# A rebuilt middle stage in a fused adaptive-layernorm block with two attentions: quotients token by token, centring on ScalarE

## What is computed

```python
phiQ, phiK = favor(Q), favor(K)                 # [B, H, T, 64]
KV, Ksum = einsum('bhtm,bhtd->bhmd', phiK, V), phiK.sum(axis=2)
out_heads = einsum('bhtm,bhmd->bhtd', phiQ, KV) / (einsum('bhtm,bhm->bht', phiQ, Ksum)[..., None] + EPS)
x = x + ga * (merge(out_heads) @ Wo.T + bo)
h = layernorm(x) * (1 + cb) + sb                # second norm, scale and shift
xn = layernorm(h) * norm_w + norm_b             # third norm, per expert
q, k, v = (xn[..., :m] @ w[:, :m].T + b for w, b in ((q_w, q_b), (k_w, k_b), (v_w, v_b)))
x = x + gb * (h + softmax(q @ k.T / 16) @ v @ o_w.T + o_b)
```

## Time and profile before

| | |
|---|---|
| median of 3 runs | 2007.24 us (2006.68 to 2007.88) |
| the profiled execution's own time | 2007.16 us |
| its span, and mean granted TensorE clock | 2005.4 us, 0.93 of 2.4 GHz |
| busy share: TensorE, VectorE, GpSimd, ScalarE | 87%, 72%, 59%, 54% |
| batch 1's middle stage, from the first L1188 to the last L911's end | 683.14 to 778.75 us: 95.6 us |
| batch 1's first score of the softmax attention | 794.51 us |

### The profile page before, as it was taken

One profiled execution on the slowest core, in us unless ns is written; L12 is line 12 of the kernel. 1 busy time (PEld: TensorE's weight loads), 2 busy tenths in 40 slices (PEclk: granted clock), 3 DMA queues, 4 the chain that ended last, 5 costly groups with the idle time before them and its releaser, 6 DMA issues.

```text
span 2005.4 us, 31471 instructions
## 1 busy us (share of the span) xinstructions
PE 1750.5 (87%) x11520; PEld 997.9 (50%) x11520; DVE 1450.5 (72%) x2617; ACT 1083.1 (54%) x1998; POOL 1179.5 (59%) x974
## 2 busy tenths in 40 slices
PE   5698869999899886999979977799997988599997
PEld 3576434444377543444447744344435764344443
DVE  4686777777478577777648857777766876787774
ACT  0586333656578432566648823266665863336564
POOL 0685354666768346566768723666676853546666
PEclk8898978999999897999989989899998989889999
DMA  4000043001110025101020003500111000430011
GB/s 126 1 2 1 18 158 85 17 11 39 53 33 2 1 72 167 30 9 48 1 85 2 2 1 117 140 12 17 41 34 52 2 2 0 171 89 16 12 37 43
DMA packets 55714, 87.56 MB, mean 44 GB/s; under 512 B 13188, under 2 KB 32004, under 8 KB 52868
## 3 DMA queue, kind: packets, MB, share of 16 engines
q1 hardware_dynamic: 55560, 85.54, 14.5%
HBM read 49.68 MB, written 35.70 MB: 43 GB/s over the span
## 4 chain that ended last, share of the span: by engine, by line
PE 65%; DVE 14%; ACT 10%; issue 4%; POOL 3%; DMA 2%; SPq 2%; POOLq 0%; ACTq 0%; DVEq 0%
PE PS L1175 12%; PE PS L1300 11%; PE PS L1288 9%; PE PS L1313 5%; PE PS L1069 5%; DVE MXP L861 4%; PE PS L1096 3%; PE PS L1077 3%; PE PS L1218 3%; PE PS L1106 3%; ACT HT L525 2%; ACT HTR L528 2%; PE PS L1245 2%; DVE QKS L911 2%; ACT PHIQ L563 2%
## 5 line engine op out<-in xcount | busy, mean ns | idle before, releaser
L498 POOL TENSOR_TENSOR TS<-PR 128x1024 f32<-128x1024 f32 (+1 forms) x256 | 573.1, 2239 | 336.7 <-ACT PR L664 336.7
L861 DVE TENSOR_REDUCE MXP<-PS 128x1 f32<-128x512 f32 x960 | 598.0, 680 | 202.7 <-PE PS L1175 199.3
L664 ACT ACTIVATE PR<-PS 128x512 f32<-128x512 f32 x960 | 504.8, 602 | 425.9 <-PE PS L1288 422.4
L1175 PE MATMUL PS<-KOP,QOP 96*128 96x512 f32 x960 | 422.8, 460 | 45.1 <-DMA KOP<-k_scr 34.2
L1288 PE MATMUL PS<-QOP,KOP 97*128 97x512 f32 x960 | 379.4, 409 | 18.1 <-ACT PR L664 12.7
L1175 PEld LDWEIGHTS PS<-KOP,QOP 96*128 96x128 f32 x960 | 190.7, 200 | 300.3 <-DVE MXP L861 174.7
L1300 PE MATMUL PS<-PR,V 128*32 128x512 f32 x1920 | 273.1, 606 | 0.0
L1288 PEld LDWEIGHTS PS<-QOP,KOP 97*128 97x128 f32 x960 | 181.3, 192 | 85.6 <-ACT PR L664 50.2
L445 POOL TENSOR_TENSOR RSTD<-VE,minus_half 128x4 f32<-128x4 f32 x32 | 33.9, 1060 | 237.6 <-DVE VE L758 237.6
L1313 PE MATMUL PS<-TS,ones 128*32 128x512 f32 x960 | 133.2, 593 | 5.4 <-POOL TS L498 5.4
L1069 PE MATMUL PS<-W1T,HTR 128*128 128x512 f32 x384 | 115.1, 438 | 21.2 <-POOL HTR L402 21.0
(11 more groups left out here) (144 smaller groups left out, 2691.0 us busy)
## 6 DMA issues: line engine op xcount, KB each, us to landing
KOP<-k_scr SPq DMA_DIRECT2D x84, 256.0 KB, 6.0
k_scr<-QKS SPq DMA_DIRECT2D x64, 256.0 KB, 2.8
QOP<-q_scr SPq DMA_DIRECT2D x180, 64.0 KB, 2.0
q_scr<-QKS SPq DMA_DIRECT2D x40, 256.0 KB, 2.8
X<-in_L_attn_x_dram SPq DMA_DIRECT2D x16, 512.0 KB, 4.8
out_dram<-X SPq DMA_DIRECT2D x16, 512.0 KB, 3.1
QOP<-MXT SPq DMA_DIRECT2D x240, 0.5 KB
KOP<-k_scr SPq DMA_DIRECT2D x48, 64.0 KB, 2.0
```

Of the source, the lines that this page charges most:

```text
L498: g.tensor_tensor(sums(k)[:, 0:len(stage)], pair[:, :, 0], pair[:, :, 1], ALU.add).then_inc(S["psum_t"], 1)
L664: a.activation(PR[:, k % 2, w, q], bank(score_bank(p, n, w, q)), ACT.Exp).then_inc(S["ex"], 1)
L861: v.tensor_reduce(MXP[:, u % 2, i, kc:kc + 1], bank(max_bank(p)), AX.X, ALU.max).then_inc(S["am_rd"], 1)
L1175: mm(bank(max_bank(p)), QOP[0:96, u % QS6, i * P:(i + 1) * P], KOP[0:96, h % KS6, kc * CH:(kc + 1) * CH], start=True, stop=True).then_inc( ...
```

## The change

Only the middle stage, its edges and a small part of the setup are changed.

- Quotients: the features become the stationary operand. For each tile of 128 tokens, eight matmuls (one for each pair of heads) with 34 moving columns (`KVW`: 32 for the numerators, 2 for the denominators) give numerators and denominators with the tokens on the partitions. VectorE takes reciprocals straight from PSUM and multiplies into `M`; TensorE transposes `M` and ScalarE copies it to `MT`. `DENS`, `NUMS`, `RB` and their transposes are gone.
- Both centrings move from VectorE to ScalarE as `scale * x + bias`; the bias `NMR = -mean * rstd` is a new small multiply on GpSimd, and `NEGM` a new small one on VectorE. The second norm's scale and shift are on GpSimd for all four chunks.
- q and k: one ScalarE write a block in place of two, and VectorE takes the low part straight from PSUM. v is copied by ScalarE; its bias is folded into the output bias `OBE` in the setup. q's scale is folded into `W2T`.
- The order: chunk `it` and chunk `it - 2` share an iteration, and the last two chunks' projections follow after the loop. The expert order is 3, 1, 0, 2 instead of 3, 0, 1, 2. Banks 5 to 7 are a ring for the projections.
- GpSimd's preparation of the output base starts after the last `QKS` low part, and the fourth result's three operations stand between the first pair sums.
- The last transposed query features use banks 0 and 1, so they need not wait for ScalarE's copies.

```diff
@@ TensorE @@
-                        for j in range(2):
-                            for q in range(4):
-                                last = mm(bank(6)[32 * q:32 * q + 32, :], DW[:, 4 * j + q], PHIQ[:, 4 * j + q, cols],
-                                          start=j == 0, stop=j == 1, tile_position=(0, 32 * q))
...
-                                last = mm(bank(4 + j)[32 * q:32 * q + 32, :], NW[:, 4 * j + q],
-                                          PHIQ[:, 4 * j + q, cols], start=True, stop=True,
-                                          tile_position=(0, 32 * q))
...
+                def numerators(s, i):
+                    n = TPC * s + i
+                    if n >= 3:
+                        pe.wait_ge(S["m"], NT * b + n - 2)
+                    for gr in range(GR):
+                        last = mm(bank(n % 3)[:, 34 * gr:34 * gr + 34], PHIQ[:, gr, n * P:(n + 1) * P], KVW[:, gr],
+                                  start=True, stop=True)
+                    last.then_inc(S["nd"], 1)
...
+                for i in range(3):
+                    numerators(0, i)
+                for it in range(NC):
+                    if it >= 2:
+                        second_transposes(it - 2)
+                    numerators(it, 3)
+                    merge(it, 0)
+                    if it >= 2:
+                        second_values(it - 2, 0)
+                    merge(it, 1)
+                    projected(it, 0)
+                    projected(it, 1)
+                    if it >= 2:
+                        second_values(it - 2, 1)
+                    if it < NC - 1:
+                        for i in range(3):
+                            numerators(it + 1, i)
+                    if it >= 2:
+                        second_qk(it - 2)
+                maxima(0, EARLY)
+                for s in (NC - 2, NC - 1):
+                    second_transposes(s)
+                    second_qk(s)
+                    second_values(s, 0)
+                    second_values(s, 1)
+                    maxima((s - NC + 3) * EARLY, (s - NC + 4) * EARLY)
...
+            for e in range(EXPERTS):
+                o, m = sum(width[:e]), width[e]
+                ks, rows = range(KD if e == 0 else 1), min(width[e], P)
+                for k in ks:
+                    last = mm(bank(3)[:, o:o + m], VBC[0:rows, k], OWT[0:rows, k, 0:m], start=k == 0,
+                              stop=k == len(ks) - 1)
+            last.then_inc(S["obm"], 1)
@@ VectorE @@
+                def quotients(s, h):
...
+                        counted = mark(v.tensor_scalar(R[:, i], nd[:, :, 32:34], FAVOR_EPS, None, ALU.add))
...
+                    first = mark(v.reciprocal(R[:, 2 * h], R[:, 2 * h]))
...
+                        v.tensor_tensor(M[:, i].rearrange("p (g h d) -> p g h d", g=GR, h=2),
+                                        nd[:, :, 0:32].rearrange("p g (h d) -> p g h d", h=2),
+                                        R[:, i].rearrange("p g (h o) -> p g h o", o=1).broadcast_to([P, GR, 2, DK]),
+                                        ALU.mult).then_inc(S["m"], 1)
...
+                for it in range(NC):
+                    quotients(it, 0)
+                    quotients(it, 1)
+                    if it >= 1:
+                        second_input(it - 1)
+                    residual(it)
+                    if it >= 2:
+                        low_parts(it - 2)
+                maxima(0, EARLY)
+                second_input(NC - 1)
+                low_parts(NC - 2)
+                maxima(EARLY, 2 * EARLY)
+                low_parts(NC - 1)
+                maxima(2 * EARLY, 3 * EARLY)
@@ GpSimd @@
+                def deviations(s, ready, signal, count):
...
+                    g.tensor_tensor(RSTD[:, cols], VE[:, cols], minus_half[:, cols], ALU.pow).then_inc(S["rs"], 1)
...
+                    g.tensor_tensor(NMR[:, cols], NEGM[:, cols], RSTD[:, cols], ALU.mult).then_inc(S[signal], 1)
...
+                for it in range(NC + 1):
+                    if it >= 1:
+                        count += 1
+                        deviations(it - 1, "ve3", "nmr3", count)
                     if it < NC:
-                        rsqrt(slot(it), "ve2", "rstd2", NC * b + it + 1)
...
+                        deviations(it, "ve2", "nmr2", count)
+                        scaled(it)
...
+                wait_all(pool, (S["q_lo"], NQ * (b + 1)))
@@ ScalarE @@
+                        a.activation(Hh[:, t], X[:, t], ACT.Identity, bias=NMR[:, t:t + 1], scale=RSTD[:, t:t + 1]
+                                     ).then_inc(S["xh2"], 1)
...
+                normal(NC - 2)
+                centred(NC - 1)
+                high_qk(NC - 2)
+                values_bank(NC - 2, 0)
+                values_bank(NC - 2, 1)
+                centred_again(NC - 1)
+                normal(NC - 1)
+                high_qk(NC - 1)
```

More of the change, by code:

```diff
@@ new lines, in merged, with normal @@
+                def merged(s, h):
+                    act.wait_ge(S["mT"], 2 * (NC * b + s) + h + 1)
+                    if s > 0:
+                        act.wait_ge(S["yps"], 2 * (NC * b + s))
+                    a.activation(MT[:, :, 2 * P * h:2 * P * (h + 1)], bank(3 + h).rearrange("p (j n) -> p j n", j=2),
+                                 ACT.Copy).then_inc(S["mt"], 1)
+                def normal(s):
+                    e = expert[s]
+                    for k in range(KD if e == 0 else 1):
+                        weight, bias = ((COLM[:, e - 2, 0:1], COLM[:, e - 2, 1:2]) if e >= 2 else
+                                        (COLS[:, 0, k:k + 1], COLS[:, 1, k:k + 1]))
+                        act.wait_ge(S["x2T"], xns(b, s) + k + 1)
+                        if s > 0:
+                            act.wait_ge(S["vp"], 2 * (NC * b + s))
+                            act.wait_ge(S["qp"], NQ * b + blocks(s)[0][0])
+                        a.activation(XNT[:, k], bank(ring(("x", s, k))), ACT.Identity, bias=bias, scale=weight
+                                     ).then_inc(S["xn_sb"], 1)
@@ new lines, in second_values @@
+                def second_values(s, h):
+                    ks = range(KD if expert[s] == 0 else 1)
+                    pe.wait_ge(S["xn_sb"], xns(b, s) + len(ks))
+                    pe.wait_ge(*freed(b, ("v", s, h)))
+                    for i in range(2):
+                        tok = slice((2 * h + i) * P, (2 * h + i + 1) * P)
+                        for k in ks:
+                            last = mm(bank(ring(("v", s, h)))[:, i * D:(i + 1) * D], XNT[:, k, tok], W2T[:, k, 2 * D:],
+                                      start=k == 0, stop=k == len(ks) - 1)
+                    last.then_inc(S["vp"], 1)
@@ new lines, in second_qk @@
+                def second_qk(s):
+                    ks = range(KD if expert[s] == 0 else 1)
+                    pe.wait_ge(S["xn_sb"], xns(b, s) + len(ks))
+                    for n, t in blocks(s):
+                        j, w = t % 2, (1 if t < 2 else 0)
+                        pe.wait_ge(*freed(b, ("q", s, n)))
+                        for k in ks:
+                            last = mm(bank(ring(("q", s, n))), W2T[:, k, w * D + j * P:w * D + (j + 1) * P], XNT[:, k],
+                                      start=k == 0, stop=k == len(ks) - 1)
+                        last.then_inc(S["qp"], 1)
```

439 lines of the change are left out of this document (199 added, 240 removed).

## The result

| | before | after |
|---|---|---|
| median, range, 5 runs each | 2007.24 us (2005.34 to 2008.23) | 2048.40 us (2044.61 to 2054.24) |
| span of the profiled execution | 2005.4 us | 2046.6 us |
| mean granted clock | 0.93 | 0.91 |

The ratio is 1.021, with a 95% interval of 1.019 to 1.023: the change makes the kernel 2.1% slower, by 41 us. The forecast was slower by 85. Sign and mechanism came as forecast, and the size is less than half.

What follows compares the result with a forecast made beforehand. TensorE, busy 87% of the span, was taken as the bound, with its clock deciding. Per batch 21.9 - 2.1 + 0.5 = 20.3 us, four times 81, plus setup 3.8, made 85 on 2007.16: 2092, range 2000 to 2112.

Steps and rivals of the forecast that it cites:

- the stretch grows by 21.9 us: Middle stage, each batch: first numerator matmul to last low part goes from 95.6 to 117.5 us, laid out chunk by chunk.
- the rest: Middle stage after chunk 3: remaining q, k and v work, last norm and low parts, laid out at 32.1 us a batch.
- four tiles at half clock: Chunk 0's numerators on TensorE all run at half clock, 13.6 us of that chunk's 22.3.
- The stream neither raises the clock nor holds it: TensorE numerators: the 34-column stream acts like the setup's 4-column one, which stayed at 0.50; likeliest case, chance 0.60.
- The pitches 0.114 and 0.213: Numerator matmuls on TensorE: us per instruction at full and half clock, set by the stationary load.
- the clock holds: Rival: numerators hold the clock but do not raise it; stretch 96.2 us a batch, 2007 in all; chance 0.12.
- the stream counts like a dense one: Rival: numerators raise the clock, chunk 0 takes 16.1 us and not 22.3, 1982 in all; chance 0.13.
- clock falls in some chunks only: Rival: the middle stage's clock falls depend on how dense work falls in between, 2020 to 2050; chance 0.10.
- The GpSimd loop: Rival: GpSimd's 13.1 us a chunk becomes the bound, 2082 as a term of its own; chance 0.05.
- The tail: End of the middle stage: five engines hand on, with a 4 us wait between chunk 2's third and fourth q blocks.
- The start: Before the numerators: last query features no longer wait for ScalarE and two small copies go, 2.1 us earlier a batch.
- The half microsecond for GpSimd's late base: Before the first pair sum: output base preparation ends 2 us late, mostly hidden; 0.5 us a batch (0 to 2.3).

Runs made afterwards that it cites:

- old_edge: The changed kernel with the last transposed query features in one bank again, each set waiting for ScalarE's copy: 2065.41 us, ratio 1.028 to before.
- w119: The changed kernel with each numerator matmul streaming 119 columns in place of 34, same results: 1983.39 us, ratio 0.986 to before.
- base: The changed kernel with GpSimd's output base preparation let go when the last centring is written, not after the last low part: 2048.59 us, ratio 1.020 to before.
- tail: The changed kernel with chunk 2's first three low parts ahead of chunk 3's second-norm statistics on VectorE: 2043.85 us, ratio 1.018 to before.

## Why the prediction was right in kind and wrong in size

- **The failed step is the layout by chunks, the term "the stretch grows by 21.9 us".** It was mis-sized by its share of half clock: the stretch grew by 42.4 us in four batches, 10.6 a batch (426.1 us against 4 x 117.5 = 470). Chunk by chunk:

| | laid out | batch 0 | batch 1 | batch 2 | batch 3 |
|---|---|---|---|---|---|
| chunk 0 | 22.3 | 18.4 | 18.4 | 18.4 | 18.4 |
| chunk 1 | 17.2 | 16.7 | 16.7 | 16.7 | 16.7 |
| chunk 2 | 20.5 | 18.5 | 16.8 | 16.8 | 16.8 |
| chunk 3 | 25.4 | 25.1 | 20.3 | 23.4 | 20.3 |
| the rest | 32.1 | 32.7 | 31.1 | 32.7 | 31.1 |

Of the 11.0 us of error a batch, on the mean, 3.9 are in chunk 0, 3.2 in chunk 2 and 3.1 in chunk 3.
- **In chunk 0 I wrote "four tiles at half clock".** The clock was 0.97 in the first 2.8 us. My evidence was a start with two waits between the transposes, and the change takes exactly these waits away; I counted their 2.1 us and not what a dense stretch does to the clock. old_edge shows the step: 13.87 us with the waits, 11.43 without.
- **In chunks 2 and 3 I let the clock return only inside `Wo`, or not at all.** In batch 1 transposes and v had brought it back by 745 (the stretch to 749 is at 1.00), so that `Wo` took 3.62 and not 5.5. In chunk 3 q and k, 4.52 at a mixed clock, brought it back before the fourth tile: 1.97 and not 3.4, and all behind it at 1.00. In batches 0 and 2 it fell once more there, and the fourth tile took 3.63, as laid out.
- **"The stream neither raises the clock nor holds it" was right**, by w119 too: with columns added and nothing else, the time fell to 1983.39. The pitches 0.114 and 0.213 hold: 5.44/48 = 0.113, 3.47/16 = 0.217 (which has the last one's own length in it).
- **The rivals.** That the clock holds fell with the stretch at 0.50 for 8.60 us. That the stream counts like a dense one fell too. Its sum, 1982, is nearly what w119 measured, in part by luck: the stretch took 91.2 us a batch there where that layout adds up to 90.0, and the start gained 3.4 and not 2.1. The range that holds the result, 2020 to 2050, belonged to "clock falls in some chunks only", which got 0.10 and no layout of its own. Its condition came in part: the clock fell in all four chunks, but in two of the four batches it was back for chunk 3's fourth tile. The GpSimd loop never was the bound: before its scale and shift (L504) GpSimd stood idle 75.4 us, 74.2 of them for ScalarE.
- **The tail** came in its size (31.1 for 32.1) and in its place: the 4.17 us between the third and fourth q block is the 4 us forecast, and L1264 waited for `M` in chunk 3 for 2.02 (1.5). In part its sum came by offsets: centring on ScalarE took 2.06 us for four tiles where I had 1.6 from a PSUM source, and a last pair of quotients 1.2 (763.35 to 764.54) where I had 1.6.
- **Smaller terms.** The start gained 3.1 a batch, not 2.1. The setup cost 2.6 of 3.8, the bias matmuls 3.66 us of TensorE; and the first stage of batch 0 took 127.8 us against 124.5, with the clock at 0.50 in 76 to 80 us where before had 1.00. That the later start moved it there isn't shown: w119, which sets out at 66.7, has 128.0 in that stage too, but `base` and `tail`, at 67.5 and 67.8, have 123.5 and 123.6. The half microsecond for GpSimd's late base is not to be seen (`base`).

Open is why batches of one execution differ by 8 us in where the clock falls: batches 0 to 3 of the change took 111.3, 103.4, 108.0 and 103.4 us in the middle.

## What to carry to other kernels

When an edit replaces a few wide matmuls by many narrow ones, price them twice: by the pitch that the stationary load sets, and by what they do to the clock of the work behind them, here 65 us in 2048. If the load sets the pitch, more moving columns can be free (here up to 119, the widest that was tried), and they can keep the clock up: try padding before a restructure is given up. And lay the clock out stretch by stretch with the waits that the edit itself takes away, since transposes and projections run densely raise it again.

## What the runs showed that I had not expected

- An f32 matmul with a 128 x 128 stationary operand takes the same time at 34 and at 119 columns, 0.113 and 0.114 us an instruction at the full clock.
- TensorE busy without a gap is no sign of a full clock: 8.60 of 8.60 us at 0.50 with 34 columns, 7.20 of 7.20 at 1.00 with 119. With 68 columns both happen in one batch (11.79 and 7.26 us for 64).
- A dense stretch of key-value matmuls and transposes raised the clock: 0.50 in 693 to 695, 0.97 in 697.2 to 700; with two waits of 0.78 and 0.69 us between the transposes it stayed at 0.50.
- A wait that an edit takes from one engine can be held by a queue elsewhere: in `tail` SP issued the store of a finished block behind nine loads, 4.13 us of issuing, and ScalarE, GpSimd's bias in hand, waited for it.
